# A layer of eight experts on sorted tokens in 23 tiles, its two weight parts loaded apart

## What is computed

```python
gate_scores = softmax(x @ Wg + bg)
top1_idx    = argmax(gate_scores)
top1_weight = sum(gate_scores * one_hot(top1_idx))
h = silu(einsum('btd,edh->bteh', x, W1) + b1)
o = einsum('bteh,ehd->bted', h, W2) + b2
y = sum(o * one_hot(top1_idx)[..., None], axis=2) * top1_weight
x = layernorm(x + y)
```

## Time and profile before

| | us |
|---|---|
| median of three runs | 6390.07 (6388.35 to 6396.14) |
| the profiled execution | 6391.87 |
| its span, first to last instruction | 6390.1 |

### The profile page before, as it was taken

The page is one execution under the profiler, slowest core; times in us unless marked ns, Lnnn a source line. Parts: engine busy times, 40 slices in busy tenths (PEclk is TensorE's granted clock), DMA queues, the critical chain, the costliest instruction groups (busy, mean ns, idle before and its releaser), DMA issues. The chain is left out here.

```text
span 6390.1 us, 128995 instructions
## 1 busy us (share of the span) xinstructions
PE 4716.8 (74%) x51675; PEld 3223.8 (50%) x51683; DVE 3581.3 (56%) x9434; ACT 1403.9 (22%) x2503; POOL 1043.7 (16%) x1087
## 2 busy tenths in 40 slices
PE   2766767667677499999887774576685577787797
PEld 1555555555555356666555552343463345565454
DVE  7889898898894300000255455588244445444445
ACT  1222222222222121121122223111133322231111
POOL 1223232232232200000122220000010012221000
PEclk7888888888889699999988886555686687888899
DMA  1110111111100100000000000000000000000000
GB/s 49 29 28 21 29 29 26 28 25 29 29 20 22 42 14 13 26 13 13 8 0 0 31 7 12 3 0 0 36 0 5 5 4 0 26 3 6 10 17 25
DMA packets 51863, 109.59 MB, mean 17 GB/s; under 512 B 5520, under 2 KB 43792, under 8 KB 49296
## 3 DMA queue, kind: packets, MB, share of 16 engines
q1 hardware_dynamic: 51344, 102.21, 5.6%
HBM read 98.78 MB, written 3.41 MB: 16 GB/s over the span
## 5 line engine op out<-in xcount | busy, mean ns | idle before, releaser
L1603 PE MATMUL psum<-arena 128*128 128x512 f32 x1600 | 706.6, 595 | 58.4 <-DVE Y L1667 35.8
L1684 DVE SCALAR_TENSOR_TENSOR Y<-psum,arena,Y 128x256 f32<-128x256 f32 x416 | 172.5, 477 | 847.9 <-PE psum L1615 847.9
L1615 PE MATMUL psum<-arena 128*128 128x256 f32 x2624 | 583.0, 380 | 4.1 <-DVE arena L1708 4.1
L754 POOL TENSOR_TENSOR weights<-weights,arena 128x64 f32<-128x64 f32 x512 | 395.7, 794 | 1042.4 <-DVE arena L1272 1042.3
L1615 PEld LDWEIGHTS psum<-arena 128*128 128x128 f32 x2624 | 499.3, 190 | 111.7 <-issue 43.5
L144 POOL TENSOR_TENSOR arena<-arena,eps 128x4 f32<-128x4 f32 (+2 forms) x76 | 16.3, 214 | 3214.1 <-DVE arena L139 3214.1
L1603 PEld LDWEIGHTS psum<-arena 128*128 128x128 f32 x1600 | 304.4, 191 | 409.1 <-issue 341.4
L1322 DVE TENSOR_TENSOR arena<-arena 128x120 f32<-128x120 f32 (+27 forms) x1888 | 398.1, 252 | 4.3 <-DVE arena L1315 2.7
L831 PE MATMUL psum<-arena 128*32 128x1 bf16 x639 | 114.2, 179 | 385.7 <-DVE arena L1284 301.1
L1315 DVE TENSOR_TENSOR arena<-arena 128x120 f32<-128x120 f32 (+27 forms) x1888 | 390.3, 246 | 6.4 <-DVE arena L1322 2.9
L422 PE MATMUL psum<-ident,arena 128*128 128x128 f32 x1280 | 217.5, 325 | 210.4 <-ACT arena L493 210.4
(11 more groups left out here) (419 smaller groups left out, 8347.5 us busy)
## 6 DMA issues: line engine op xcount, KB each, us to landing
weights<-L_decay_rows SPq DMA_DIRECT2D x256, 160.0 KB, 3.5
arena<-in_experts_L_ffn SPq DMA_DIRECT2D x8, 2052.0 KB, 7.5
arena<-in_ctxT SPq DMA_DIRECT2D x16, 512.0 KB, 3.2
arena<-in_experts_L_ffn SPq DMA_DIRECT2D x18, 384.0 KB, 3.0
weights<-in_w_L_ffn SPq DMA_DIRECT2D x1, 3072.0 KB, 9.9
weights<-in_w_L_attn SPq DMA_DIRECT2D x1, 2881.0 KB, 12.9
weights<-in_w_L_ffn SPq DMA_DIRECT2D x1, 2753.0 KB, 11.8
weights<-in_w_L_relu SPq DMA_DIRECT2D x1, 2436.0 KB, 9.1
```

What stands on the lines that cost most here:

```text
L754: a = pool.tensor_tensor(blocks, bc(w.minus_eye, 1, 2), bc(beta[:, at, 2 * b:2 * b + 2], 2, Q), ALU.mult)
L1603: mm = nc.tensor.matmul(ps[:, bank, :], W[s][name][:, c, f * P:(f + 1) * P], xT[:, g, c, :], start=(c == 0), stop=(c == C - 1))
L1615: mm = nc.tensor.matmul(out, h[:, m % 2, f, u * P:(u + 1) * P], W[s]["w2"][:, f, :], start=(f == 0), stop=(f == FC - 1))
```

## The change

The table RUN calls a new function for "L0_ffn". After the routing, the kernel counts how many tokens each expert has, and gives each token a row in a list sorted by expert, where each expert's part begins at a multiple of 128 rows. 2048 tokens and eight experts fit in 16 + 7 = 23 tiles of 128 rows whatever the routing; rows without a token hold zeros. POOL writes the 16 tiles of X to those rows in DRAM with 16 indirect DMAs. For each of the 23 tiles the number of its expert is read from SBUF into a register, its weights are loaded, in two parts, the rows are loaded and transposed, and the two products are made with 128 tokens and that one expert. The part with W1 and b1 goes through SP's queue (`load_weights`), the part with W2 and b2 through ScalarE's (`load_down`), in its instruction order between the activations of two tiles. There are three buffers for weights, tokens and results. b2 enters as a ninth product of one row. VectorE copies the result out of PSUM, SP stores it, and when all are stored POOL fetches the rows back in the tokens' order with 16 indirect DMAs. Then VectorE adds them to X with the weight of each token, and normalises; POOL's square roots stand behind the 16 fetches in its order. All loops are written out; the last stage keeps `experts_stage`.

The new function is cut to its core here:

```diff
--- before.py
+++ after.py
+def dispatched_experts_stage(k):
...
+    E, FC = 8, 1024 // P
+    SLOTS = B + E - 1
+    BUFS = 3
...
+    UP = C * FC * P + FC
...
+    x_sorted = nc.dram_tensor("L0_ffn_x_sorted", (SLOTS * P, D), F32).ap()
+    y_sorted = nc.dram_tensor("L0_ffn_y_sorted", (SLOTS * P, D), F32).ap()
+
+    ew = A(BUFS, words)
+    xs, xT, h, y = A(BUFS, D), A(2, C, P), A(2, FC, P), A(BUFS, D)
...
+    T_BANK, UP_BANK, Y_BANK = 0, 1, 5
...
+        @block.sync
+        def _(sp):
+            sp.wait_ge(consts_set, 1)
+            sp.dma_start(x_sorted.rearrange("(s p) d -> p s d", p=P), bc(zeros, 1, SLOTS)).then_inc(zeroed, 16)
+            sp.wait_ge(placed, 2)
+
+            def load_weights(s):
+                if s >= BUFS:
+                    sp.wait_ge(down_ready, s - BUFS + 1)
+                e = sp.value_load(owner_i[0:1, s:s + 1], min_val=0, max_val=E - 1)
+                sp.dma_start(ew[:, s % BUFS, 0:UP], streamed[bass.ds(e, 1), :, 0:UP].rearrange("a p n -> p (a n)")
+                             ).then_inc(w_arrived[s % BUFS], 16)
+
+            def load_x(s):
+                if s >= BUFS:
+                    sp.wait_ge(x_turned, s - BUFS + 1)
+                sp.dma_start(xs[:, s % BUFS, :], x_sorted[s * P:(s + 1) * P, :]).then_inc(x_arrived[s % BUFS], 16)
+
+            def store_y(s):
+                sp.wait_ge(y_ready, s + 1)
+                sp.dma_start(y_sorted[s * P:(s + 1) * P, :], y[:, s % BUFS, :]).then_inc(y_stored[s % BUFS], 16)
+
+            for s in range(BUFS):
+                load_weights(s)
+            sp.wait_ge(scattered, 16 * B)
+            for s in range(BUFS):
+                load_x(s)
+            for s in range(BUFS, SLOTS):
+                load_x(s)
+                load_weights(s)
+                store_y(s - BUFS)
+            k.prefetch(sp, stage)
+            for s in range(SLOTS - BUFS, SLOTS):
+                store_y(s)
...
+            turned.stage(pool, 0)
+            for g in range(TURNS - 1):
+                turned.stage_next(pool, g)
+            pool.wait_ge(placed, 1)
+            pool.wait_ge(zeroed, 16)
+            for b in range(B):
+                pool.indirect_dma_start(x_sorted, bass.IndirectOffsetOnAxis(ap=position_i[:, b:b + 1], axis=0),
+                                        k.X[:, b, :], None).then_inc(scattered, 16)
+            for i in range(BUFS):
+                pool.wait_ge(y_stored[i], 16 * len(range(i, SLOTS, BUFS)))
+            for b in range(B):
+                pool.indirect_dma_start(gathered_y[:, b, :], None, y_sorted,
+                                        bass.IndirectOffsetOnAxis(ap=position_i[:, b:b + 1], axis=0)
+                                        ).then_inc(gathered[b // TILES], 16)
+            for g in range(TURNS):
+                norm.roots(pool, g)
...
+            pe.wait_ge(chosen, 1)
+            flat = onehot.rearrange("p b e -> p (b e)")
+            nc.tensor.matmul(ps[:, 1, 0:B * E], w.earlier, flat, start=True, stop=True)
+            nc.tensor.matmul(ps[:, 1, B * E:2 * B * E], ones, flat, start=True, stop=True).then_inc(counted, 1)
+            pe.wait_ge(placed, 1)
+
+            def turn_tile(s):
+                pe.wait_ge(x_arrived[s % BUFS], 16 * nth(s))
+                if s:
+                    pe.wait_ge(x_ready, s)
+                for c in range(C):
+                    mm = nc.tensor.transpose(ps[:, T_BANK, c * P:(c + 1) * P], xs[:, s % BUFS, c * P:(c + 1) * P],
+                                             k.ident)
+                mm.then_inc(x_turned, 1)
+
+            def up(s):
+                pe.wait_ge(w_arrived[s % BUFS], 16 * nth(s))
+                pe.wait_ge(x_ready, s + 1)
+                for f in range(FC):
+                    n = s * FC + f
+                    if n >= 4:
+                        pe.wait_ge(h_ready, n - 3)
+                    for c in range(C):
+                        mm = nc.tensor.matmul(ps[:, UP_BANK + f % 4, 0:P], W[s % BUFS]["w1"][:, c, f * P:(f + 1) * P],
+                                              xT[:, s % 2, c, :], start=(c == 0), stop=(c == C - 1))
+                    mm.then_inc(up_ready, 1)
+
+            def down(s):
+                pe.wait_ge(h_ready, (s + 1) * FC)
+                pe.wait_ge(w2_arrived[s % BUFS], 16 * nth(s))
+                if s >= 2:
+                    pe.wait_ge(y_ready, s - 1)
+                out = ps[:, Y_BANK + s % 2, 0:D]
+                nc.tensor.matmul(out, ones[0:1, :], W[s % BUFS]["b2"][0:1, :], start=True, stop=False)
+                for f in range(FC):
+                    mm = nc.tensor.matmul(out, h[:, s % 2, f, :], W[s % BUFS]["w2"][:, f, :], start=False,
+                                          stop=(f == FC - 1))
+                mm.then_inc(down_ready, 1)
+
+            turn_tile(0)
+            for s in range(SLOTS):
+                up(s)
+                if s + 1 < SLOTS:
+                    turn_tile(s + 1)
+                if s:
+                    down(s - 1)
+            down(SLOTS - 1)
...
+            nc.scalar.activation(router.scores, router.scores, ACT.Exp).then_inc(exp_ready, 1)
+            act.wait_ge(placed, 2)
+
+            def load_down(s):
+                if s >= BUFS:
+                    act.wait_ge(down_ready, s - BUFS + 1)
+                e = act.value_load(owner_i[0:1, s:s + 1], min_val=0, max_val=E - 1)
+                act.dma_start(ew[:, s % BUFS, UP:], streamed[bass.ds(e, 1), :, UP:].rearrange("a p n -> p (a n)")
+                              ).then_inc(w2_arrived[s % BUFS], 16)
+
+            for s in range(BUFS - 1):
+                load_down(s)
+            for s in range(SLOTS):
+                for f in range(FC):
+                    act.wait_ge(up_ready, s * FC + f + 1)
+                    if f == 0 and s >= 2:
+                        act.wait_ge(down_ready, s - 1)
+                    nc.scalar.activation(h[:, s % 2, f, :], ps[:, UP_BANK + f % 4, 0:P], ACT.Silu,
+                                         bias=W[s % BUFS]["b1"][:, f:f + 1]).then_inc(h_ready, 1)
+                if s + BUFS - 1 < SLOTS:
+                    load_down(s + BUFS - 1)
...
+            router.top1(dve, chain, lg).then_inc(chosen, 1)
+
+            dve.wait_ge(counted, 1)
+            counts = ps[:, 1, B * E:2 * B * E].rearrange("p (b e) -> p e b", e=E)
+            chain(dve.tensor_copy(totals, counts))
...
+            dve.tensor_copy(position_i, position).then_inc(placed, 1)
+            chain(dve.tensor_tensor(past, bc(ends[:, 0:E - 1], 1, SLOTS), bc(w.slots, 2, E - 1), ALU.is_le))
+            chain(dve.tensor_reduce(owner, past, AX.X, ALU.add))
+            dve.tensor_copy(owner_i, owner).then_inc(placed, 1)
+            dve.wait_ge(exp_ready, 1)
+            chain(dve.tensor_reduce(router.a[:, 0:B], router.scores, AX.X, ALU.add))
+            chain(dve.reciprocal(weight, router.a[:, 0:B]))
+
+            def take_x(s):
+                dve.wait_ge(x_turned, s + 1)
+                if s >= 2:
+                    dve.wait_ge(up_ready, (s - 1) * FC)
+                dve.tensor_copy(xT[:, s % 2, :, :], ps[:, T_BANK, 0:D].rearrange("p (c t) -> p c t", t=P)
+                                ).then_inc(x_ready, 1)
+
+            def take_y(s):
+                dve.wait_ge(down_ready, s + 1)
+                if s >= BUFS:
+                    dve.wait_ge(y_stored[s % BUFS], 16 * (nth(s) - 1))
+                dve.tensor_copy(y[:, s % BUFS, :], ps[:, Y_BANK + s % 2, 0:D]).then_inc(y_ready, 1)
+
+            take_x(0)
+            for s in range(SLOTS):
+                if s + 1 < SLOTS:
+                    take_x(s + 1)
+                if s:
+                    take_y(s - 1)
+            take_y(SLOTS - 1)
+
+            for g in range(TURNS):
+                dve.wait_ge(gathered[g], 16 * TILES)
+                for u in range(TILES):
+                    b = g * TILES + u
+                    norm.add(dve, chain, g, u, gathered_y[:, b, :], factor=weight[:, b:b + 1])
+                norm.moments(dve, chain, g)
+                norm.apply(dve, chain, g)
+    sem.release()
...
 PACKS["L0_ffn"] = lambda i: dict(wg=by_rows(i["L0_ffn_Wg"]), bg=row(i["L0_ffn_bg"]), before=before_matrix(8),
-                                 b2=np.concatenate([np.asarray(i["L0_ffn_b2"]), np.zeros((P - 8, D), np.float32)]))
+                                 earlier=np.triu(np.ones((P, P), np.float32), 1), slots=row(np.arange(B + 7, dtype=np.float32)))
...
     E = w1.shape[0]
+    b2 = np.zeros((E, P, D), np.float32)
+    b2[:, 0, :] = np.asarray(i["L0_ffn_b2"])
     return {"experts_L0_ffn": np.ascontiguousarray(flat_experts(
-        w1.reshape(E, C, P, -1).transpose(0, 2, 1, 3), w2.reshape(E, -1, P, D).transpose(0, 2, 1, 3),
-        b1.reshape(E, -1, P).transpose(0, 2, 1)))}
+        w1.reshape(E, C, P, -1).transpose(0, 2, 1, 3), b1.reshape(E, -1, P).transpose(0, 2, 1),
+        w2.reshape(E, -1, P, D).transpose(0, 2, 1, 3), b2))}
...
```

(2 more changed lines are left out.)

88 lines of the change are left out of this document (added).

## The result

The changed kernel takes 5755.66 us (four runs, 5747.46 to 5758.93), the kernel before 6393.10 beside it: a ratio of 0.9001, 95% interval 0.8985 to 0.9017. The forecast was 5747, range 5700 to 5870. The profiled execution took 5754.96, 8.0 more than the forecast (7.8 before the forecast was rounded).

What follows compares the result with a forecast made beforehand. The prediction took PE, without slack at full clock, to bound the expert stage. Its terms summed to 327.8 us instead of 972.5, 644.7 less, taking the profiled 6391.9 to 5747 us, range 5700 to 5870.

Steps and rivals of the forecast that it cites:

- loop: The 23 expert tiles: 23 x 8.3 = 190.9 us, plus 4.0 for a first tile at half speed, 194.9 together.
- closing: End of the stage after normalisation, taken to be as before: 1.0 us.
- The second product has 9 (one for b2), so 18 records at 0.218: 3.9 us: PE work of each tile's second product, part of the 7.9 us of PE work taken per tile.
- the period is the mean of the two: Loop: load arrival 8.3 to 9.2 us after release and PE work 7.9 average to 8.1 to 8.55; 8.3 taken.
- let both queues share: Loop's weight loads: SP's and ScalarE's queues share the 16 engines, so the first part lands after 7.5 to 8.4 us.
- alternative of independent queues: Loop's weight loads: with independent queues the first part lands like 1159 KB, period 7.9, total 9 us lower at 5738.
- The indirect transfers: POOL's 16 scatter and 16 gather transfers: 1.5 us each taken, between 0.34 and 2.92.
- Their rival: Scatter and gather: 32 serial indirect transfers make the kernel slower than before, from 21.6 us each; chance 0.03.
- Weights late: Rival in the loop: loads pace it at a period of 12, 85 us more, total 5832; chance 0.12.
- ScalarE is held: Rival in the loop: register read and issue take 3 us, PE waits about 1.8 a tile, total 5788; chance 0.09.
- this cover is thin: ScalarE's load between tiles: 1.6 of PE's 1.8 us of room is used; each us more costs one per tile.
- Low clock: Rival in the loop: PE at 1.2 GHz throughout, 15.8 us a tile, 172 us more, total 5919; chance 0.06.

Runs made afterwards that it cites:

- e_no_b2: The changed kernel without the ninth product, so b2 is not added and each tile has less PE work: 5755.61 us against 5755.66.
- e_sp_both: The changed kernel with both weight parts on SP's queue, the first part ahead, and no load issued by ScalarE: 5742.53 us against 5755.66.
- e_hold: The changed kernel with ScalarE reading the expert's number three times instead of once before each second-part load: 5765.16 us against 5755.66.

## Why the prediction was right, and where it was off

The reason given held: PE was the bound at full clock, the number of products was cut by the program itself, and the new serial work was small. By its own terms:

| term | predicted | measured | from |
|---|---|---|---|
| routing | 44.8 | 44.6 | 2196.93 to 2241.54 |
| counting | 4.8 | 5.0 | to the last of VectorE's positions, 2246.53 |
| scatter | 26.0 | 22.6 | to the tokens' load at 2269.12 |
| first tokens | 3.6 | 3.6 | to 2272.72 |
| loop | 194.9 | 207.5 | to 2480.20 |
| last copy and store | 2.9 | 3.0 | to 2483.18 |
| gather | 24.0 | 19.9 | to POOL's first root at 2503.12 |
| normalisation | 25.8 | 25.8 | to 2528.94 |
| closing | 1.0 | 2.0 | to 2530.89 |
| sum | 327.8 | 334.0 | |

**The term that was mis-sized is the loop**, by 12.6 us. Two steps of it failed. "The second product has 9 (one for b2), so 18 records at 0.218: 3.9 us" charged b2's product as one of nine; the pair occupies 0.63, not 0.44. That is 0.19 of the 0.25 by which the PE work of an unstalled tile, 8.15 (2280.11 to 2288.26), exceeds the 7.9 taken; most of the rest is the sixteen other records, 3.56 instead of 3.49. 23 x 0.25 is 5.8 us. The other step is "the period is the mean of the two". The measured excess over PE's work is 8.83 - 8.15 = 0.68 a tile against the 0.4 taken (8.3 - 7.9): 23 x 0.28 = 6.4. With the measured 8.15 and 9.0 the rule gives 8.58, an excess of only 0.43. What it left out is that the landings differ, from 7.5 to 9.6 us and once 5.3, and that a late one costs its full length while an early one gains nothing: followed on paper as for e_no_b2, the loop has a period of 8.76 with the 20 recorded landings, an estimate that comes near the 8.83. The two steps make 12.2 of the 12.6; the rest of the loop, mainly the first tile's slow products (6.62 against 3.83) and the one slow product at the end (5.46), is 207.5 - 23 x 8.83 = 4.4, where 4.0 was taken.

The number for the load itself was good: 0.70 for waking and reading the register (0.8 taken) and 8.3 to land (7.5 to 8.4), 9.0 after the release. It was reached by "let both queues share", and that is what happened. What the prediction did not ask is what the sharing costs: e_sp_both shows that the same bytes in the order of need give 4.9 for the first part, and the pair at 2378.00 that a lead of 0.28 us does nearly as well.

The rule of the Trainium skill, "DMA: Bandwidth & Descriptors", section "Issuing engines are not separate DMA queues", agrees with these runs: two queues moved the parts no faster (8.3 and 8.4) than one queue moved the whole (8.6). No run supports the alternative of independent queues, by which a period of 7.9 was worked out.

**The indirect transfers** were taken at 1.5 and cost 1.26 in the scatter and 1.25 in the gather (0.96 busy and 0.30 to the next); 16 of each gave back 3.4 and 4.1 of the loop's error. That the sum is off by only 6.2 is thus partly luck: the errors have opposite signs. Their rival, 21.6 us each, was far off.

**The rivals of the loop.** *Weights late* came true in kind and not in size: an excess of 0.68 a tile instead of the rival's 12 - 7.9 = 4.1. *ScalarE is held* did not come, but "this cover is thin" was right, as e_hold shows. *Low clock* did not come: the granted clock was 1.00, the upper level of 2.4 GHz, from 2290 to 2450 in spite of ten waits of up to 1.90 us there. It dipped once, after the wait ahead of 2458.12, where that tile's first product took 5.46 instead of 3.84 and the window shows 0.85. By the rule of the Trainium skill, "TensorE: Matmul & The Clock Gate", section "HAM oscillation — how this bites in real kernels", the total would have been 5919; the waits of this loop are shorter than those which that section describes, and the trace does not show its pattern, a fall of the clock at every slice. But the rival was not far away: in e_no_b2 waits of 1.85 to 2.87 us were followed by four such dips.

**The closing** took 1.0 more than taken: the idle time ahead of the last L117 is 1.95 after the change and 1.18 ahead of the stage. Its cause was not sought.

## What to carry to other kernels

Where two transfers serve one tile and one is needed first, let that one leave first, on one queue in the order of need or a few tenths of a us ahead: from two issuing engines at the same moment they are moved side by side, and the urgent one lands as late as the other. Release each part of a buffer by the last instruction that reads that part. Before work is saved on an engine that waits for loads, look whether the loads can follow, and look at the granted clock afterwards: in e_no_b2 longer waits brought slower products, and the saving was lost. And behind a long run of transfers on one engine's queue, look for the small operation that another engine waits for: moving such operations forward gave 8.7 us here.

## What was not expected of the hardware

- Two transfers that leave on two queues within 0.03 us of each other land nearly together (1028 KB after 8.3 us, 1152 KB after 8.4). A lead of 0.28 us is enough to change this: 5.3 for the first, 7.8 for the other. With 1.05 us of lead it is 5.1 (e_hold).
- Taking 0.82 us of PE work per tile from a loop that waits for its loads every other tile gained nothing per tile (8.83 to 8.84): the waits grew, and after four of them, of 1.85 to 2.87 us, the first product ran 1.5 to 1.6 us longer at a granted clock of 0.83 in that window.
- A product of one row of weights (b2's, 1 x 128 by 256 columns) occupies PE for 0.63 us in its two records, counted to the start of the next product, more than the 0.44 of two records with 128 rows.
- Reading one word into a register costs about 0.52 us of an engine's sequence.
- An indirect transfer of 128 rows of 1 KB takes POOL 1.25 us of its sequence, writing or reading.
